# A two-layer graph network on one core: setup loads all issued by SP, transposes and attention products in turn, and sums cleared by ScalarE

## The reference

```python
xp = (x @ W).reshape(N, H, C)                   # x: 3125 x 1024, W: 1024 x 1024, H = 4
a_src = jnp.einsum('nhc,hc->nh', xp, att_src)
a_dst = jnp.einsum('nhc,hc->nh', xp, att_dst)
e = jax.nn.leaky_relu(a_src[src] + a_dst[dst], 0.2)
# softmax of e over the edges of each dst, weighted sum of xp[src], + bias, relu
```

## Time and profile before

| | |
|---|---|
| median of 3 runs | 2373.01 us (2373.01 to 2373.22) |
| profiled execution | 2372.47 us, span 2370.2 us, mean granted clock 0.946 |
| order block | 0 to 23.6 us |
| setup block | 23.6 to 128.2 us |
| logit stage with the scan | 128.2 to about 597 us |

### The profile page before, as it was taken

One profiled execution on the slowest core, in us unless ns is written; L12 is line 12 of the kernel. 1 busy time (PEld: TensorE's weight loads), 2 busy tenths in 40 slices (PEclk: granted clock), 3 DMA queues, 4 the chain that ended last, 5 costly groups with the idle time before them and its releaser, 6 DMA issues. The chain is left out here.

```text
span 2370.2 us, 50338 instructions
## 1 busy us (share of the span) xinstructions
PE 1858.2 (78%) x10714; PEld 1234.4 (52%) x10715; DVE 1615.5 (68%) x4084; ACT 850.7 (36%) x2910; POOL 1408.1 (59%) x1472
## 2 busy tenths in 40 slices
PE   2979989876688888888769957777777763899797
PEld 2634434433466666666557745555555542666543
DVE  3546555539666666666679956666666567999987
ACT  1300000001677777777657640000000002555364
POOL 1177777772777777777601147777777762666600
PEclk8989999998899999999979989999999996999899
DMA  8133223220899999999899837888888864777466
GB/s 317 42 89 90 70 70 74 66 56 9 308 357 361 356 359 360 361 356 359 307 303 318 291 101 227 244 234 245 231 248 237 238 191 145 239 253 253 154 196 224
DMA packets 253495, 529.81 MB, mean 224 GB/s; under 512 B 52189, under 2 KB 144998, under 8 KB 253370
## 3 DMA queue, kind: packets, MB, share of 16 engines
q0 software_dynamic: 97472, 275.27, 35.6%
q1 hardware_dynamic: 118051, 209.21, 26.7%
q10 hardware_dynamic: 37878, 44.27, 6.8%
HBM read 439.07 MB, written 102.49 MB: 228 GB/s over the span
## 5 line engine op out<-in xcount | busy, mean ns | idle before, releaser
L1211 ACT ACTIVATE wone<-onehot,w 128x64 f32<-128x64 f32 x1760 | 432.2, 334 | 145.0 <-DVE onehot L1257 141.3
L155 POOL DMA_INDIRECT acc<-xl_table,csrc x392 | 401.8, 1025 | 124.7 <-issue 104.5
L155 POOL DMA_INDIRECT ga<-a_src_table,csrc x316 | 317.0, 1003 | 122.4 <-issue 79.4
L1228 PE MATMUL banks<-w_sb,wone 128*64 128x256 f32 x2368 | 315.8, 392 | 72.2 <-DMA w_sb<-xp_table,isrc 43.5
L942 PE MATMUL banks<-w_sb,acc 128*128 128x512 f32 x768 | 362.4, 616 | 0.0
L155 POOL DMA_INDIRECT w_sb<-xp_table,isrc x296 | 294.9, 996 | 90.1 <-issue 49.4
L1253 DVE TENSOR_TENSOR acc<-banks,acc 128x512 f32 x440 | 304.4, 692 | 0.0
L1689 PE MATMUL banks<-xr_parts,onehot_t 128*128 x1320 | 187.8, 286 | 130.3 <-issue 97.4
L1821 PE MATMUL banks<-msg,onehot 128*128 128x265 f32 x880 | 215.8, 398 | 37.5 <-POOL msg L1791 17.8
L1717 DVE SCALAR_TENSOR_TENSOR prod<-banks,att_relu 128x1024 f32<-128x1024 f32 x110 | 134.7, 1224 | 157.6 <-ACT w L1653 157.6
L1689 PEld LDWEIGHTS banks<-xr_parts,onehot_t 128*128 128x128 bf16 x1320 | 127.3, 96 | 214.0 <-issue 175.0
(11 more groups left out here) (325 smaller groups left out, 2758.8 us busy)
## 6 DMA issues: line engine op xcount, KB each, us to landing
edge_rows<-acc SPq DMA_DIRECT2D x440, 130.0 KB
rows<-edge_rows SPq DMA_DIRECT2D x55, 1040.0 KB, 4.9
lt_bc<-local_dst ACTq DMA_DIRECT2D x110, 128.0 KB, 3.8
lt<-local_dst ACTq DMA_DIRECT2D x110, 128.0 KB, 4.3
xp_table<-xp_st SPq DMA_DIRECT2D x25, 512.0 KB, 3.0
w<-acc SPq DMA_DIRECT2D x100, 128.0 KB, 3.8
xpt<-xp_table SPq DMA_DIRECT2D x25, 512.0 KB, 5.4
x_table<-y POOLq DMA_DIRECT2D x25, 512.0 KB, 6.7
```

Source lines behind the costliest of these rows:

```text
L155: return self.pool.indirect_dma_start(out, None, table, bass.IndirectOffsetOnAxis(ap=idx, axis=0), bounds_check=self.bound, oob_is_err=False)
L1211: last = nc.scalar.activation(wone[:, s, j, h, :], onehot[:, s, j, :], ACT.Copy, scale=w9[:, bass.ds(g * U + j, 1), h:h + 1].rearrange("p ...
L1228: nc.tensor.matmul(psum[WN * a:WN * (a + 1), j, k * C:(k + 1) * C], wone[:, s, j, h, :], slots[r][:, j, h * C:(h + 1) * C], start=True, st ...
```

## The change

- x is loaded by SP in the setup block, all 13 pairs in order, behind the twelve edge loads (L547 to L565); ACT issues nothing in the first two blocks, and `first_x` is gone.
- PE transposes tiles in the order 0 to 24. After 18 tiles (LED = 9 pairs), products and transposes take turns: two pairs of products, two tiles. The edge transposes (`sources`) come ahead of pair 8, the sums of tiles 0 to 15 ahead of pair 11, those of tiles 16 to 24 at the end. The table of source logits is stored in two parts, and `s_as` counts 32.
- Tile 0's product with W is cut up: k 0 to 1 ahead of the edge rows' transposes, k 2 to 3 behind them, k 4 to 7 in the logit stage ahead of the first look-up.
- EARLY is 1 instead of 3, so 4 gathers are in the setup block and the rest in the logit stage.
- POOL's three memsets at the end of the logit stage are gone; ACT clears `zacc` and the 14 tiles with activations of scale 0, after its loads and once 22 tiles' products are done.

```diff
-        EARLY = 3
+        EARLY = 1
+        FIRST_K = 4
...
-            def load_x(act, pairs):
-                for p in pairs:
+            def load_x(sp):
+                sp.wait_ge(s_pad, 4)
+                for p in range(NPAIR):
...
-            def first_x(act):
-                load_x(act, PAIRS_FIRST[:-1])
-                act.wait_ge(s_pad, 4)
-                load_x(act, PAIRS_FIRST[-1:])
...
+            def in_turn(tile, pair, middle, late):
+                for t in range(2 * LED):
+                    tile(t)
+                for p in range(NPAIR):
+                    if p == 8:
+                        middle()
+                    if p == 11:
+                        late()
+                    pair(p)
+                    if p % 2:
+                        for t in range(2 * LED + p - 1, min(2 * LED + p + 1, NT)):
+                            tile(t)
...
@@ setup block, gpsimd
-                    pool.wait_ge(s_as, 16)
+                    pool.wait_ge(s_as, 32)
                     fetch_sources(pool, range(EARLY))
@@ setup block, sync
                     assert n_edge + 2 == N_EDGE_DMAS
+                    load_x(sp)
                     sp.wait_ge(s_ct, 1)
                     sp.dma_start(edge_t.rearrange("(b p) n -> p b n", b=NB), ...)
...
+                        for i, tiles in enumerate((slice(0, HALF), slice(HALF, NT))):
+                            sp.wait_ge(s_all, i + 1)
+                            sp.dma_start(as_rows[:, tiles, :], a_all[:, tiles, 0:H]).then_inc(s_as, 16)
@@ setup block, tensor
+                    in_turn(transposes, products_a, sources, lambda: sums(0, range(HALF)))
+                    sums(1, range(HALF, NT))
+                    first_tile(0, 2)
+                    pe.wait_ge(s_all, 2)
                     pe.wait_ge(s_lw, 1)
                     for i, rows in enumerate((lrow, sv0, fv, wrow)):
...
+                    first_tile(2, FIRST_K)
                     pe.wait_ge(s_tq, 4)
@@ logit stage, gpsimd
-                    gather = fetch_sources(pool, range(EARLY, len(FETCHED) + 2))
-                    gather.wait(s_fetched, NGC)
-                    gather.wait(s_xp, NU)
-                    nc.gpsimd.memset(zacc[:], 0.0)
-                    nc.gpsimd.memset(acc[:, 0:KEPT, :], 0.0)
-                    nc.gpsimd.memset(acc[:, KEPT + 8:NU, :], 0.0)
+                    fetch_sources(pool, range(EARLY, len(FETCHED) + 2))
@@ logit stage, scalar
+                    def clear(sums):
+                        nc.scalar.activation(sums, bc(pidx[:], [P, sums.shape[1]]), ACT.Copy, scale=0.0)
+                    clear(zacc[:].rearrange("p t n -> p (t n)"))
+                    act.wait_ge(s_xp, NU)
+                    for t in [*range(KEPT), *range(KEPT + 8, NU)]:
+                        clear(acc[:, t, :])
@@ logit stage, tensor
+                    for k in range(FIRST_K, KD):
+                        for i in range(2):
+                            last = nc.tensor.matmul(psum[:, i], xT_all[:, 0, k, :], w_sb[:, k, i * 512:(i + 1) * 512],
+                                                    start=False, stop=(k == KD - 1))
+                    last.then_inc(s_xp, 1)
```

More of the change, by code:

```diff
@@ L253, in _ @@
                 sp.wait_ge(s_copy, 32)
-            @block.scalar
-            def _(act):
-                first_x(act)
             @block.tensor
@@ L395, in gnn_kernel @@
             W_FIRST = 3
[L396 to L399, removed]
+            LED = 9
+            HALF = 16
+            assert 5 * KEYS + EC <= (NT - 1) * D
             def chunk_rows(name, words=P):
@@ L608, in _, with transposes @@
                     pe.wait_ge(s_ident, 2)
-                    for q, t in enumerate(TILES):
+                    def transposes(t):
                         pe.wait_ge(s_xi[t // 2], 16)
-                        wait(pe, s_xT, q - 1)
-                        if q == 14:
+                        wait(pe, s_xT, t - 1)
+                        if t == 14:
                             pe.wait_ge(s_lastw, 1)
@@ L639, in _ @@
                         last.then_inc(s_am, 1)
[L640 to L649, removed]
@@ L650, in _, with sources @@
-                    last.then_inc(s_xp, 1)
-                    pe.wait_ge(s_all, 1)
-                    pe.wait_ge(s_csrc, 1)
+                    def sources():
+                        pe.wait_ge(s_ci, 1)
+                        pe.wait_ge(s_low, 1)
+                        for b in range(NB):
+                            nc.tensor.transpose(psum[:, 7, b * TB:(b + 1) * TB], ct[:, b, 0, :], ident[0:TB, 0:TB])
+                            last = nc.tensor.transpose(psum[:, 5, b * TB:(b + 1) * TB], hi[:, b, :], ident[0:TB, 0:TB])
+                        last.then_inc(s_cs, 1)
@@ new lines, in sums @@
+                    def sums(i, tiles):
+                        pe.wait_ge(s_csrc, 1)
+                        pe.wait_ge(s_ac, tiles[-1] // 2 + 1)
+                        for t in tiles:
+                            last = nc.tensor.matmul(psum[:, 5 + 2 * i, (t - tiles[0]) * 2 * H:(t - tiles[0] + 1) * 2 * H],
+                                                    aT[:, t // 2, (t % 2) * P:(t % 2 + 1) * P], summed[:],
+                                                    start=True, stop=True)
+                        last.then_inc(s_at, 1)
@@ new lines, in first_tile @@
+                    def first_tile(k0, k1):
+                        for k in range(k0, k1):
+                            for i in range(2):
+                                nc.tensor.matmul(psum[:, i], xT_all[:, 0, k, :], w_sb[:, k, i * 512:(i + 1) * 512],
+                                                 start=(k == 0), stop=False)
+                    in_turn(transposes, products_a, sources, lambda: sums(0, range(HALF)))
+                    sums(1, range(HALF, NT))
+                    first_tile(0, 2)
@@ L911, in _ @@
                     for i in range(4):
-                        nc.scalar.activation(acc[:, KEPT + i, :], bc(pidx[:], [P, D]), ACT.Copy, scale=0.0)
+                        clear(acc[:, KEPT + i, :])
                 @block.tensor
```

59 lines of the change are left out of this document (28 added, 31 removed).

## The result

The changed kernel takes 2340.43 us (median of 4 runs, 2337.57 to 2344.49) against 2373.01 us before (median of 4 runs, 2369.38 to 2373.22), 32.6 us less. The forecast was 2348 in a range of 2341 to 2360. The profiled execution is the slowest of the four (2344.49, span 2342.8 at a granted clock of 0.953).

The account below looks back on a forecast made before the run. POOL's gathers were taken to pace the logit stage, with a stall at its end. POOL resuming 24.1 us earlier, less 10.6 of added work, plus 11.8 of stall, gave 25.3 us gained: forecast 2348 us, range 2341 to 2360.

Parts of the forecast that it names:

- rival C: Setup: SP's edge loads take as long as before and x stands behind them; 2382 us, slower by 9; chance 0.04.
- DVE's chain ends (`ab`): Setup: edge table's store 5.5 us, gathers 7.5 and 10.4 from `csrc` to `ab`, after 67.4, end at 91.
- rival E: Setup: order block over sooner, x evenly spread, chains overlap; POOL at 99, 2341 us or a little less; chance 0.08.
- The memset stall: Logit stage's end: taking the memsets off POOL frees DVE's copy, 11.8 us gained, with ACT's clears hidden.
- Rival B: Logit stage's end: the stall stays, through another wait or ACT's clears reaching over L891; 2360 us; chance 0.04.
- D: Setup gains nothing that reaches POOL, which resumes at 129.57; 2372 us, no change; chance 0.04.
- The start: Setup's start: flag at 8, order block's end at 15, edge DMAs issued by about 24, x moving from 27 us.
- The tail of x on one engine: Setup: the 53-row last x load runs on one engine for about 8 us and lands at 69.
- PE's chain: Setup on PE: from 55, transposes, products, sums and a quarter of tile 0's product take 36.8 us, to 91.8.
- rival A: Setup: PE stays at its low clock while x trickles in; 2355 to 2360 us; chance 0.15.
- The end of the setup: Setup's end: 12.7 us from the edge rows' transposes at 92.5 to POOL resuming, at 105.5.
- The stage: Logit stage: eight gathers and two ticks moved in by EARLY 3 to 1 add 10.6 us.

Follow-up runs that it names:

- e8: The kernel before with the same PE work left out as in e7 and ACT's clears in place of POOL's memsets: 2355.33 us, ratio 0.9935.
- e7: The kernel before with seven of eight k slices of each logit-stage product and most of the source look-up left out: 2368.19 us, ratio 0.9989.
- e3: The changed kernel with the 13 x loads issued by ACT instead of SP, on a slow chip: 2962.52 us against 2973.53, ratio 0.9957.
- e12: The same kernel as e3, x loads issued by ACT, on another slow chip: 2963.28 us against 2975.43, ratio 0.9961.
- e4: The changed kernel with all 25 tiles transposed before the first product (LED = 13), on a slow chip: 2961.62 us against 2973.53, ratio 0.9947.
- e11: The changed kernel with EARLY 3 instead of 1 (12 gathers in the setup), on a slow chip: 2946.62 us against 2975.43, ratio 0.99.
- e9: The changed kernel with the same PE work left out of the logit stage as in e7: 2335.74 us, ratio 0.9849.
- e6: The changed kernel itself run again, unaltered, on a fast chip: 2340.78 us against 2370.21 before, ratio 0.9868.
- e10: The changed kernel with edge rows' transposes ahead of tile 0's early matmuls, only 8 of them in the setup; slow chip: 2951.72 us, ratio 0.9926.
- e5: The kernel before with ACT's clears in place of POOL's memsets, on a slow chip: 2992.52 us against 3002.36, ratio 0.9974.

## Why the prediction came out

| step | predicted | measured |
|---|---|---|
| flag, end of the order block | 8, 15 | 8.45, 15.17 |
| SP held in an edge load (rival C) | no | 3.45 us at most |
| x under way, tile 17 done | 27, 55 | transposes from 29.96, about 52.9 |
| `wa` done | 46 | 41.4 |
| `st` gathers begin | 72.9 | 69.43 |
| DVE's chain ends (`ab`) | 91 | 87.8 |
| edge rows' transposes | 91.8 to 92.5 | 91.68 |
| POOL resumes | 105.5 | 101.65 |
| added to the stage | 10.6 | 9.42 |
| stall gone | 11.8 | 11.76 |
| at the scan | 25.3 | 30.26 |

The forecast missed low in the direction of rival E (more than I think, POOL at 99, 2341 or a little less), to which it gave a chance of 0.08; POOL's 101.65 lies between the forecast and that rival.

**The memset stall** was right to 0.1 us, and its cover by ACT too; e8 against e7 isolates it. Rival B is out, and with POOL 27.92 us sooner D as well.

**The start** came out as forecast: `near`, with nothing ahead of it, came early, the block again ended 6.7 us behind the flag, and no edge load was held for more than 3.45 us. No run puts x back into the order block alone, so that x made `near` late is argued and not isolated. Rival C is out, and e3 and e12 show that it was a real danger: with x on a second queue SP is held for 14 us.

**The tail of x on one engine** was there. From 62 to 69 us the DMA view of the changed kernel has this queue:

```profile
q1 hardware_dynamic: 100, 0.16, 6.1%
```

6.1% of sixteen engines is one engine, at 22 to 25 GB/s. The rule of the Trainium skill (DMA: Bandwidth & Descriptors, section "Why a DMA increments its semaphore by 16 and not by 1"), by which 53 rows go to one engine, agrees with it. The tail cost nothing here, because products fill PE up to 69.40; where they don't, in e4, PE stood 4.83 us for it.

**PE's chain** came out right in sum and not in its parts. It began 2 us sooner (52.9) and took 38.8 us instead of 36.8. That its end was met to 0.1 us is luck, since two misses of 2 us cancel. The clock was 0.67 in 75 to 90 us. The sums took 7.72 us, as forecast, and a quarter of tile 0's product 5.70 us instead of 3.9: those 1.8 us are nearly all of the 2.0. The forecast had a quarter of the 15.8 us that 32 matmuls took before, but those didn't run at one pace: the trace before has 0.77 in 95 to 102.5 us, under the sums, 0.52 in 102.5 to 106, behind them, and 1.00 from there on. The fall was there to be read, and the first quarter should have been priced at the low clock. In e11 and e9 the clock of 75 to 90 us was 0.89; in e11 the same quarter took 3.68 us, the edge rows' transposes stood at 87.28 and POOL's first source gather at 88.10 instead of 90.66. So the low clock was worth some 4 us. This is rival A's price, in a place that I hadn't named: not while x trickles in (1.00 in 15 to 75 us), but behind the sums.

**The end of the setup** is the term that was mis-sized. I took 12.7 us from the edge rows' transposes to POOL's next gather; it was 9.97. I had put 1.6 us on the twelve gathers, the time by which the last of them ended behind DVE, and nothing on what comes after it. The end of the block before:

```profile
123.75 0.60 DVE L788 CAST tabs<-banks 1x440 int32<-1x440 f32 x1
...
124.93 1.00 POOL L155 DMA_INDIRECT ga<-a_src_table,csrc  x1 [0.30 <-issue]
...
128.19 0.38 SPq L861 DMA_DIRECT2D bias_bc<-in_L_gnn_bias  x1
```

The next block's first issues stood 3.84 us behind DVE's end at 124.35 and 2.26 us behind POOL's last gather; after, DVE ended the block and the next began 0.26 us later. e11 puts the gathers back and has 2.33 us again. So the gathers had held the block for some 3.6 us and not 1.6, which is 2.0 of the missing 2.7 us. The extra quarter, at nearly the full clock, lengthened PE's part by 1.98 us (from 4.65 to 6.63) instead of 2.6, and POOL's first gather came 1.20 us into the block instead of 1.38.

One sum of this part was wrong without effect: 88 + 7.8 + 5.2 is 101.0 for POOL's own four gathers and not 101.5.

**The stage** grew by 9.42 us instead of 10.6: 312 x 1.325 against 304 x 1.329. The idle time put down to waits on the gathers' DMAs stayed the same (12.5 against 12.8 us). The same eight gathers made the stage 9.9 us longer in e9 than in e7 and 10.9 longer than in e8 (413.29 against 403.35 and 402.43), so 10.6 lies among the measured values and the 1.2 us among their differences.

Together: POOL resumed 3.85 us ahead of the forecast (0.8 from the edge rows' transposes, 2.7 from the setup's end, 0.3 that I had rounded up), and the stage gave 1.2. That is 5.0 of the 7.3 us by which the medians' difference beats the sum; the other 2.3 are within what the stages behind the scan vary from one execution to the next.

## What to carry to other kernels

When one engine bounds a stage, look at what sets its start and at what it does behind its last useful instruction: here POOL's start moved by 27.9 us through the order of loads three engines away, and its last act, a memset, cost 12 us through DVE. Here one queue in order of need, issued by an engine that had nothing else to do, beat two queues at once by 12 to 15 us, since the second queue held up small loads on the first (14.4 us) and the issuing engine's own work (25.5 us). Interleave work that has its data with work that waits for a transfer's tail. When POOL's gathers end a block, count what comes behind the last of them (2.3 us here) and set it against the 1.3 us that each gather made there saves in a stage that POOL bounds. And price matmuls at the clock of the place where they will stand, not at their mean: the stretch behind the small sums was at the low clock before the change as well.

## What the runs showed of the hardware

**A chain of short POOL memsets can shut DVE out as one long memset does.** DVE's 128x16 copy took 12.05 us beside two large memsets (10.35 and 1.81 us) and was over with the second. Beside fourteen small ones (0.94 us each) one such copy took 0.87 us and the next 8.14, until the last memset was over. ACT's clears of the same tiles held nothing: the two such copies that fell beside them in the changed kernel took 0.17 us each.

**PE's clock fell behind small matmuls.** From 75 to 90 us PE was busy for 14.2 to 14.5 of 15 us, yet the granted clock was 0.67 (changed, e6), 0.60 (e10) and 0.89 (e9, e11); in e4, where products filled that stretch up to 83.4, it was 1.00 and fell later. What went before each fall were the 96x8 sums: the eight 128x512 matmuls behind them took 5.4 to 5.8 us in six executions (changed, e3, e4, e6, e9, e12) and 3.68 in e11, where the clock was back in time. No run takes the sums away, so that they are the cause is argued.

**Two kinds of chip.** On three of the chips the kernel before takes 2973 to 3002 us; each chip was used at one time only, so a difference of the chip and one of the hour aren't told apart. Busy time by stretch, first the changed kernel (fast kind), then e5 (slow kind):

```profile
128.00:300.00 172.00, 158.03 (x636) 72.76 (x635) 93.66 (x432) 0.00 (x0) 133.66 (x163) 0.98 0.33 77
```

```profile
128.00:300.00 172.00, 53.95 (x133) 21.47 (x134) 20.01 (x81) 0.94 (x2) 121.90 (x150) 0.57 0.14 26
...
620.00:720.00 100.00, 100.00 (x417) 46.46 (x416) 63.44 (x291) 0.00 (x0) 0.00 (x0) 1.00 0.30 88
```

While POOL gathers, PE starts a fifth of the matmuls and DVE works for a fifth of its former time; when POOL's gathers are over (its last tick is at 560.53) PE goes at full pace, and the scan begins 300 us later than elsewhere. Between single matmuls PE stands for 1 to 3 us, and the profile puts it down to issue, a wait for nothing that it shows:

```profile
321.05 1.01 PE L944 MATMUL banks<-w_sb,acc 128*128 128x512 f32 x1 [1.79 <-issue]
```

From 128 to 520 us of e5 these short waits are 52.5 us; another 164.4 us are 17 waits ahead of the destination look-ups (45.2 us the longest), also put down to issue, and ACT takes 95.10 us for five DMA issues in a row. So it isn't PE alone that is slow to start. The setup is longer by 3 us at most. What the cause is isn't shown, nor that the gathers are it; they only go together in time. On these chips POOL's end doesn't decide and the memset stall is worth nothing. Last ticks at 551.14 (e12), 537.62 (e10) and 533.62 (e11) go with 2963.28, 2951.72 and 2946.62 us on one chip, three points that differ in more than the tick.
